# Last stage: a bank of its own for one sum, and another order of ScalarE's and VectorE's steps

## The chip, the cores and the metric

One Trainium2 chip; the kernel runs on one core. The time is the device time of the whole program in microseconds (us), the median of three runs. TensorE (PE) multiplies matrices into PSUM, eight banks of 128 x 512 fp32; VectorE (DVE) and ScalarE (ACT) read and empty them; GpSimd (POOL) and SyncE (SP) mostly issue transfers. Each engine runs its own list of instructions in order, and they wait for each other with semaphores.

## What is computed

The reference is two graph layers and two mixtures of experts over 10,000 rows of 512 features. The last stage is the second mixture, eight experts with 32 hidden units each, of which the two best count for a row:

```python
def _L1_ffn_ref(x, router_w, w1, b1, w2, b2, gamma, beta):
    logits = xf @ router_w
    gate_vals, idx = jax.lax.top_k(logits, K)        # K = 2
    gates = jax.nn.softmax(gate_vals, axis=-1)
    out = jnp.zeros_like(xf)
    for e in range(E):                               # E = 8
        h = jax.nn.relu(xf @ w1[e] + b1[e]) @ w2[e] + b2[e]
        y = _layernorm(xf + h, gamma[e], beta[e])
        w = jnp.sum(jnp.where(idx == e, gates, 0.0), axis=-1)
        out = out + w[:, None] * y
    return out.reshape(B, S, D)
...
    x = x + _L1_gnn_ref(_layernorm(x), ...)
    x = x + _L1_ffn_ref(_layernorm(x)[None], ...)[0]
    return x
```

## The kernel before

The last stage is `dense1_phase`. The rows are cut into 20 chunks `g` of 512 rows, each of four tiles `t` of 128 rows; the last chunk has three tiles. A fully unrolled loop of 21 rounds (`bodies`, `body(0, c_)`) runs on every engine, with the order of the steps written out by hand for each. In round `g` four chunks are in work: `front` is chunk g+2, whose rows are made ready (`scale_y`, `sum_`, `square`, variance); `mid` is chunk g+1, which is normalised (`norm`), turned by TensorE (`turn`), and split into a high and a low half (`high` on ScalarE, `low` on VectorE); `main` is the inner chunk g, with the hidden units (`up`, `hidden`, `hidden_high`, `hidden_low`), the variances of the experts (`cross`, `gram`, `quadratic`, `turn_squares`, `sum_squares`) and the routing; `behind` is chunk g-1, whose coefficients are made, turned and spread (`turn_coef`, `spread`, `scale`, `weighted_high`, `weighted_low`) and whose result is made (`product` on TensorE, `finish` on VectorE: a multiplication with `pox[t]` and an addition of `po1[t]`). `in_range` switches the four parts off at the ends. Every wide matmul is done in three (`split3`, lines 67 to 69), with high and low halves.

A product of 512 floats by 128 partitions fills a PSUM bank, and all eight are taken: `pu0`, `pu1`, `pq0`, `pq1`, `ptr`, `psm`, `pb`, `px`. From chunk 1 on all four turns of a chunk's rows use the one bank `ptr` (`turn_bank`): the turn of tile t+1 waits until tile t's low half is made (`xl_made`). The fourth tile's product uses the same two banks as the second's, `pb` and `px`, and waits for the second tile's `finish` (line 3424). The lists of `body` that matter: ScalarE's, from line 3003, and VectorE's, from line 3246.

The router's logits of the next chunk come out of `logits` (8 matmuls into `psm`), which waits for all four low halves. ScalarE's `small_copy` empties that bank, `turn_small` turns it, and `logits_of` reads it on VectorE. The variance of chunk g+2 (`variance_of`, line 3122) waits for all four of ScalarE's `square`; GpSimd's `power` follows it, and VectorE's `shifts` that. In the round, VectorE does `sum_squares`, `shifts`, `finish` 0, `variance`, `logits_of` and `finish` 1 to 3 after `variance_of`, in this order, and then `coefficients` and `routing` of the next round; ScalarE starts each round's work with `softmax_exp` (line 3001), which waits for the second step of `routing`.

Of the kernel before, what the change touches and what calls it, by code (L numbers as in the profile page):

```python
# [71 lines left out]
def tiles(g):  # L72

    return LAST if g == NG - 1 else T
# [2700 lines left out]
def dense1_phase(nc, a, k, ex, out):  # L2775
# [5 lines left out]
    with ExitStack() as stack:  # L2781
# [27 lines left out]
        coef_t = c.sb("coef_t", [P, GR], F32R)  # L2809
        pu, pq = ([c.ps(f"{n}{i}") for i in range(2)] for n in ("pu", "pq"))  # L2810
        ptr, psm, pb, px = (c.ps(n) for n in ("ptr", "psm", "pb", "px"))
        pox, po1 = [pu[0], pb, pq[0], pb], [pu[1], px, pq[1], px]

        NSHIFT, NCOEF, NVAR, NROUTE, EXP_STEP = 5, 8, 4, 10, 2
        consts, first_means = c.sem("consts"), c.sem("first_means")
# [27 lines left out]
        def in_range(i, c_, ahead):  # L2843

            return not isinstance(i, int) or 0 <= c_ + ahead < NG
# [82 lines left out]
        def _(act_):  # L2928
# [14 lines left out]
            def scale_y(i, c_, t):  # L2943

                g, u = i * XS + c_, c_ % XS
                act_.wait_ge(y_in[u][t], i * 16 + 16 * (c_ // XS + 1))
                if t == 0:
                    act_.wait_ge(gains, g + 1)
                act_.activation(x3[u][:, t, :], x3[u][:, t, :], ACT.Copy, scale=gain[:, t:t + 1]).then_inc(affine, 1)
# [25 lines left out]
            def high(g, n, t):  # L2975
                act_.wait_ge(turned, 4 * g + t + 1)
                act_.activation(xh[n][:, :, t * P:t * P + P], turn_bank(g, t)[:].rearrange("p (c n) -> p c n", n=P), ACT.Copy)\
                    .then_inc(xh_made, 1)
# [5 lines left out]
            def hidden_high(g, n, fc):  # L2984
                act_.wait_ge(hid_made, FC1 * g + fc + 1)
                act_.activation(hh[:, fc, cols(g)], hid[n][:, fc, cols(g)], ACT.Copy).then_inc(hh_made, 1)
# [5 lines left out]
            def small_copy(g):  # L2992
                act_.wait_ge(small_done, g + 1)
                for b, rows in enumerate((slice(0, HALF_P), slice(HALF_P, P))):
                    act_.activation(small_t[rows].rearrange("p (a n) -> p a n", a=2),
                                    psm[rows].rearrange("p (a b n) -> p a b n", a=2, b=2)[:, :, b, :], ACT.Copy)\
                        .then_inc(small_out, 1)
# [5 lines left out]
            def body(i, c_):  # L3003
                g, n, n1 = i * XS + c_, c_ % 2, (c_ + 1) % 2
                front, mid, main, behind = (in_range(i, c_, ahead) for ahead in (2, 1, 0, -1))
                if mid:
                    norm(i, c_ + 1, 0)
                    norm(i, c_ + 1, 1)
                if c_ == 0:
                    for t in range(T):  # L3010
                        half(i, 2, t)
                if main:
                    softmax_exp(g)
                    hidden(g, n, 0)
                if mid:
                    high(g + 1, n1, 0)
                if main:
                    hidden_high(g, n, 0)
                if mid:
                    norm(i, c_ + 1, 2)  # L3020
                    if tiles(g + 1) == T:
                        norm(i, c_ + 1, 3)
                if front:
                    scale_y(i, c_ + 2, 0)
                if main:
                    hidden(g, n, 1)
                    hidden_high(g, n, 1)
                if behind:
                    act_.wait_ge(coef_turned, g)
                    act_.activation(coef_t[:], px[:], ACT.Copy).then_inc(coef_out, 1)  # L3030
                if mid:
                    high(g + 1, n1, 1)
                if front:
                    scale_y(i, c_ + 2, 1)
                    scale_y(i, c_ + 2, 2)
                if mid:
                    high(g + 1, n1, 2)
                if behind:
                    weighted_high(g - 1, 0)
                if front:  # L3040
                    if tiles(g + 2) == T:
                        scale_y(i, c_ + 2, 3)
                    square(i, c_ + 2, 0)
                    square(i, c_ + 2, 1)
                if mid and tiles(g + 1) == T:
                    high(g + 1, n1, 3)
                if behind:
                    weighted_high(g - 1, 1)
                if front:
                    square(i, c_ + 2, 2)  # L3050
                    if tiles(g + 2) == T:
                        square(i, c_ + 2, 3)
                if mid:
                    small_copy(g + 1)
                if in_range(i, c_, 3):
                    for t in range(tiles(g + 3)):
                        half(i, c_ + 3, t)
# [25 lines left out]
        def _(v):  # L3083
# [162 lines left out]
            def body(i, c_):  # L3246
                g, n, n1 = i * XS + c_, c_ % 2, (c_ + 1) % 2
                front, mid, main, behind = (in_range(i, c_, ahead) for ahead in (2, 1, 0, -1))
                if behind:
                    coefficients(g - 1, n1, (c_ - 1) % XS)  # L3250
                if front:
                    mean_of(i, c_ + 2)
                if main:
                    routing(g, n)
                if mid:
                    low(g + 1, n1, 0)
                if main:
                    hidden_low(g, n, 0)
                if front:
                    sum_(i, c_ + 2, 0)  # L3260
                if main:
                    hidden_low(g, n, 1)
                if mid:
                    low(g + 1, n1, 1)
                if front:
                    sum_(i, c_ + 2, 1)
                if behind:
                    scale(g - 1, n1, 0)
                if mid:
                    low(g + 1, n1, 2)  # L3270
                if main:
                    quadratic(g, n, 0)
                if behind:
                    weighted_low(g - 1, 0)
                if front:
                    sum_(i, c_ + 2, 2)
                    if tiles(g + 2) == T:
                        sum_(i, c_ + 2, 3)
                if mid and tiles(g + 1) == T:
                    low(g + 1, n1, 3)  # L3280
                if behind:
                    scale(g - 1, n1, 1)
                if main:
                    quadratic(g, n, 1)
                if behind:
                    weighted_low(g - 1, 1)
                if front:
                    variance_of(i, c_ + 2)
                    if in_range(i, c_, 3):
                        gains_of(i, c_ + 3)  # L3290
                if main:
                    sum_squares(g, 0)
                    sum_squares(g, 1)
                if front:
                    shifts(i, c_ + 2)
                if behind:
                    finish(i, c_ - 1, 0)
                if main:
                    variance(g, n)
                if mid:  # L3300
                    logits_of(g + 1, n1)
                if behind:
                    for t in range(1, tiles(g - 1)):
                        finish(i, c_ - 1, t)
# [37 lines left out]
        def _(pe):  # L3342
            pe.wait_ge(consts, 6)

            def turn(g, t):
                pe.wait_ge(normed, 4 * g + t + 1)
                if g:
                    pe.wait_ge(xl_made, 4 * g + t)
                for kc in range(KC):
                    last = pe.transpose(turn_bank(g, t)[:, kc * P:kc * P + P], xf[:, t, kc * P:kc * P + P], k.ident[:])  # L3350
                last.then_inc(turned, 1)
# [63 lines left out]
            def product(g, t, main):  # L3415
                sl = slice(t * P, t * P + P)
                if t == 0:
                    pe.wait_ge(cl_made, FC1 * g + FC1)
                    if main:
                        pe.wait_ge(hid_made, FC1 * g + 2 * FC1)  # L3420
                if t == 2 and main:
                    pe.wait_ge(quad_summed, FC1 * g + 2 * FC1)
                if t == 3:
                    pe.wait_ge(mul_done, 8 * g + 4 + 16)
                pe.matmul(pox[t][:], coef_t[:, sl], ex.rows_x[:], start=True, stop=True).then_inc(x_done, 1)
                pe.matmul(po1[t][:], coef_t[:, sl], ex.rows_1[:], start=True, stop=False, skip_group_check=True)
                for fc in range(FC1):
                    last = split3(pe, po1[t][:], (ch[:, fc, sl], cl[:, fc, sl]),
                                  (ex.w2g[0][:, fc, :], ex.w2g[1][:, fc, :]), False, fc == FC1 - 1)
                last.then_inc(one_done, 1)  # L3430
# [157 lines left out]
```

## Time and profile before

| | us |
|---|---|
| median of 3 runs (lowest, highest) | 2427.51 (2425.49, 2428.58) |
| the profiled execution: its time | 2430.37 |
| the profiled execution: span from first to last instruction | 2428.6 |
| PE busy | 2278.6 (94%) |
| PE weight loads busy | 1824.9 (75%) |
| DVE busy | 1795.1 (74%) |
| ACT busy | 1152.4 (47%) |
| POOL busy | 676.4 (28%) |

The last stage takes from about 1881 to the end, some 547 us. Busy shares say how much of the span an engine executes something; matmuls overlap, so TensorE's share is not a share of its peak. In the timelines the number behind the start is the length of an operation as the profiler shows it; the next operation of the same engine may start before it has ended. The bracket at a row's end tells how long the engine was idle before and what ended that.

### The profile page before, as it was taken

How to read it: one execution, taken by the hardware profiler on the slowest of the kernel's cores; microseconds unless marked ns; L12 is line 12 of the kernel's file. 1: busy time of each engine (PE TensorE's matmuls, PEld its weight loads, DVE VectorE, ACT ScalarE, POOL GpSimd, SP SyncE). 2: the span in 40 equal slices, each digit the busy share in tenths (PEclk: the TensorE clock that was granted, in tenths of full speed). 3: DMA queues.
4: the chain of work that ended last, by engine and by line, in shares of the span. 5: the costliest groups of instructions: out<-in, count | busy, mean ns of one | idle time of the engine just before them, and what ended most of it. 6: DMA issues, size and time to landing. Idle time of an engine off the chain costs nothing. (4 is left out here: it accounts for less than half of the span.)

```text
span 2428.6 us, 33166 instructions
## 1 busy us (share of the span) xinstructions
PE 2278.6 (94%) x10610; PEld 1824.9 (75%) x10610; DVE 1795.1 (74%) x4258; ACT 1152.4 (47%) x2136; POOL 676.4 (28%) x624
## 2 busy tenths in 40 slices
PE   6799986899999999999789999999997899999998
PEld 4577664688888888888668788888876677777776
DVE  8588796888888888887556755555566688888886
ACT  7565422445455454554442222222235767667652
POOL 6455022222122221210232222122133434333310
PEclk9899987999999999999899999999999899999999
DMA  5221133132231322311453343433446566666631
GB/s 168 57 54 53 19 126 104 57 100 83 75 104 53 105 70 87 102 51 52 135 173 126 125 145 127 134 129 128 135 157 195 123 174 160 148 169 166 152 106 51
DMA packets 155873, 271.89 MB, mean 112 GB/s; under 512 B 35538, under 2 KB 36178, under 8 KB 155478
## 3 DMA queue, kind: packets, MB, share of 16 engines
q1 hardware_dynamic: 123014, 203.00, 25.1%
q0 software_dynamic: 32720, 67.19, 12.9%
q8 instruction: 68, 1.11, 0.2%
q14 instruction: 71, 0.58, 0.1%
HBM read 185.82 MB, written 100.41 MB: 118 GB/s over the span
## 5 line engine op out<-in xcount | busy, mean ns | idle before, releaser
L2417 ACT ACTIVATE conv_h<-conv_h 128x512 f32<-128x512 f32 x79 | 50.0, 632 | 305.9 <-DVE conv_h L2346 288.8
L2894 POOL DMA_INDIRECT next_own<-message,net_slot_d x75 | 123.7, 1650 | 155.4 <-DMA next_own<-own 138.1
L2315 DVE TENSOR_TENSOR conv_yl<-conv_pty,conv_yh 128x512 fp32r<-128x512 f32 x79 | 54.6, 692 | 150.2 <-ACT conv_yh L2407 140.9
L67 PE MATMUL conv_p<-conv_w_hi,conv_yh 128*128 128x512 f32 x316 | 132.2, 418 | 1.2 <-DVE conv_yl L2315 1.2
L1372 POOL TENSOR_TENSOR d_rs<-d_ve,net_half_neg 128x4 f32<-128x4 f32 x37 | 37.3, 1008 | 340.8 <-DVE d_ve L1430 283.4
L67 PE MATMUL d_po<-shared_wq_hi,d_hh 128*128 128x512 f32 x316 | 129.4, 409 | 0.0
L67 PE MATMUL d_pc<-d_xh,shared_wv_hi 128*128 128x512 f32 (+1 forms) x320 | 128.4, 401 | 0.0
L67 PE MATMUL d_pa<-d_xh,xp_w_hi 128*128 128x512 f32 (+1 forms) x320 | 127.6, 399 | 0.0
L69 PE MATMUL conv_p<-conv_w_hi,conv_yl 128*128 128x512 f32 x316 | 126.2, 399 | 0.0
L68 PE MATMUL conv_p<-conv_w_lo,conv_yh 128*128 128x512 f32 x316 | 126.0, 399 | 0.0
L69 PE MATMUL conv_p<-conv_w_hi,conv_hl 128*128 128x512 f32 x316 | 125.5, 397 | 0.0
L68 PE MATMUL conv_p<-conv_w_lo,conv_hh 128*128 128x512 f32 x316 | 124.5, 394 | 0.0
L67 PE MATMUL conv_p<-conv_w_hi,conv_hh 128*128 128x512 f32 x316 | 124.2, 393 | 0.2 <-DVE conv_hl L2315 0.2
L69 PE MATMUL d_pa<-d_xh,xp_w_lo 128*128 128x512 f32 (+1 forms) x320 | 124.3, 388 | 0.0
L69 PE MATMUL d_pc<-d_xh,shared_wv_lo 128*128 128x512 f32 (+1 forms) x320 | 124.1, 388 | 0.0
L68 PE MATMUL d_pa<-d_xl,xp_w_hi 128*128 128x512 f32 (+1 forms) x320 | 123.6, 386 | 0.0
L68 PE MATMUL d_pc<-d_xl,shared_wv_hi 128*128 128x512 f32 (+1 forms) x320 | 123.4, 386 | 0.0
L69 PE MATMUL d_po<-shared_wq_hi,d_hl 128*128 128x512 f32 x316 | 123.4, 390 | 0.0
L68 PE MATMUL d_po<-shared_wq_lo,d_hh 128*128 128x512 f32 x316 | 123.3, 390 | 0.0
L1023 POOL DMA_INDIRECT early_val<-values,net_slot_s x79 | 80.8, 1022 | 122.4 <-DVE d_x L1508 56.6
L2343 DVE SCALAR_TENSOR_TENSOR conv_h<-conv_p,conv_dg,conv_msg 128x512 f32<-128x512 f32 x79 | 59.3, 751 | 70.9 <-PE conv_p L69 47.6
L2286 POOL COPY conv_at<-net_slot_d 128x4 int32 (+1 forms) x20 | 4.7, 237 | 367.8 <-DVE conv_h L2346 346.7
(621 smaller groups left out, 7209.5 us busy)
## 6 DMA issues: line engine op xcount, KB each, us to landing
conv_yin<-y SPq DMA_DIRECT2D x79, 256.0 KB, 2.8
h<-conv_h SPq DMA_DIRECT2D x79, 256.0 KB, 2.0
own<-xp_own_buf SPq DMA_DIRECT2D x79, 256.0 KB, 2.0
next_own<-own SPq DMA_DIRECT2D x79, 256.0 KB, 4.3
next_x<-y SPq DMA_DIRECT2D x79, 256.0 KB, 3.8
out<-d_res SPq DMA_DIRECT2D x79, 256.0 KB, 2.7
y<-d_y SPq DMA_DIRECT2D x78, 256.0 KB
d_x<-in_x SPq DMA_DIRECT2D x10, 1024.0 KB, 7.3
```

What stands on the lines that cost most here:

```text
L67: te.matmul(out, lhs[0], rhs[0], start=first, stop=False, skip_group_check=True)
L68: te.matmul(out, lhs[0], rhs[1], start=False, stop=False, skip_group_check=True)
L69: return te.matmul(out, lhs[1], rhs[0], start=False, stop=last, skip_group_check=True)
L1023: pool.indirect_dma_start(early.val[:, t, :], None, k.values[:, :], bass.IndirectOffsetOnAxis(ap=k.slot["s"][:, T * g + t:T * g + t + 1], ...
L1372: pool.tensor_tensor(rs[n][:], ve[n][:], k.half_neg[:, 0:T], ALU.pow).then_inc(pow_done[n], 1)
L2286: pool.tensor_copy(at[:], k.slot["d"][:, ds(T * g, T)]).then_inc(at_made, 1)
L2315: v.tensor_tensor(lo[:, t % 2, :], bank[t % 2][:], hi[:, t % 2, :].bitcast(F32), ALU.subtract)\
L2343: v.scalar_tensor_tensor(h[:, t, :], p1[t % 2][:], dg[:, t:t + 1], msg[:, t, :], ALU.mult, ALU.add)\
L2417: act_.activation(h[:, t, :], h[:, t, :], ACT.Relu).then_inc(h_made, 1)
L2894: pool.indirect_dma_start(own[n][:, t, :], None, k.message2[:, :], bass.IndirectOffsetOnAxis(ap=k.slot["d"][:, T * g + t:T * g + t + 1], a ...
```

## The change

The fourth tile's second sum, `po1[3]`, goes into the bank `ptr` instead of `px`. The fourth tile's `product` waits for one step of `finish` less (only `pb` must be free), and the first turn of a chunk, from chunk 3 on, waits for the last `finish` of the chunk three before it. On ScalarE the second tile's high half comes ahead of the coefficients' copy and of the inner chunk's second `hidden_high`; the fourth tile's comes ahead of squares 0 and 1; `small_copy` comes ahead of square 3. On VectorE the second tile's low half and `sum_` 1 come ahead of the inner chunk's second `hidden_low`, and `sum_` 3 goes from before the fourth low half to just before the variance. No operation is added or taken away.

```diff
--- before.py
+++ after.py
@@ -2809,7 +2809,7 @@
         coef_t = c.sb("coef_t", [P, GR], F32R)
         pu, pq = ([c.ps(f"{n}{i}") for i in range(2)] for n in ("pu", "pq"))
         ptr, psm, pb, px = (c.ps(n) for n in ("ptr", "psm", "pb", "px"))
-        pox, po1 = [pu[0], pb, pq[0], pb], [pu[1], px, pq[1], px]
+        pox, po1 = [pu[0], pb, pq[0], pb], [pu[1], px, pq[1], ptr]
 
         NSHIFT, NCOEF, NVAR, NROUTE, EXP_STEP = 5, 8, 4, 10, 2
         consts, first_means = c.sem("consts"), c.sem("first_means")
@@ -3024,12 +3024,13 @@
                     scale_y(i, c_ + 2, 0)
                 if main:
                     hidden(g, n, 1)
-                    hidden_high(g, n, 1)
+                if mid:
+                    high(g + 1, n1, 1)
                 if behind:
                     act_.wait_ge(coef_turned, g)
                     act_.activation(coef_t[:], px[:], ACT.Copy).then_inc(coef_out, 1)
-                if mid:
-                    high(g + 1, n1, 1)
+                if main:
+                    hidden_high(g, n, 1)
                 if front:
                     scale_y(i, c_ + 2, 1)
                     scale_y(i, c_ + 2, 2)
@@ -3040,18 +3041,19 @@
                 if front:
                     if tiles(g + 2) == T:
                         scale_y(i, c_ + 2, 3)
+                if mid and tiles(g + 1) == T:
+                    high(g + 1, n1, 3)
+                if front:
                     square(i, c_ + 2, 0)
                     square(i, c_ + 2, 1)
-                if mid and tiles(g + 1) == T:
-                    high(g + 1, n1, 3)
                 if behind:
                     weighted_high(g - 1, 1)
                 if front:
                     square(i, c_ + 2, 2)
-                    if tiles(g + 2) == T:
-                        square(i, c_ + 2, 3)
                 if mid:
                     small_copy(g + 1)
+                if front and tiles(g + 2) == T:
+                    square(i, c_ + 2, 3)
                 if in_range(i, c_, 3):
                     for t in range(tiles(g + 3)):
                         half(i, c_ + 3, t)
@@ -3258,12 +3260,12 @@
                     hidden_low(g, n, 0)
                 if front:
                     sum_(i, c_ + 2, 0)
-                if main:
-                    hidden_low(g, n, 1)
                 if mid:
                     low(g + 1, n1, 1)
                 if front:
                     sum_(i, c_ + 2, 1)
+                if main:
+                    hidden_low(g, n, 1)
                 if behind:
                     scale(g - 1, n1, 0)
                 if mid:
@@ -3274,8 +3276,6 @@
                     weighted_low(g - 1, 0)
                 if front:
                     sum_(i, c_ + 2, 2)
-                    if tiles(g + 2) == T:
-                        sum_(i, c_ + 2, 3)
                 if mid and tiles(g + 1) == T:
                     low(g + 1, n1, 3)
                 if behind:
@@ -3285,6 +3285,8 @@
                 if behind:
                     weighted_low(g - 1, 1)
                 if front:
+                    if tiles(g + 2) == T:
+                        sum_(i, c_ + 2, 3)
                     variance_of(i, c_ + 2)
                     if in_range(i, c_, 3):
                         gains_of(i, c_ + 3)
@@ -3346,6 +3348,8 @@
                 pe.wait_ge(normed, 4 * g + t + 1)
                 if g:
                     pe.wait_ge(xl_made, 4 * g + t)
+                if g > 2 and t == 0:
+                    pe.wait_ge(mul_done, 8 * (g - 3) + 8 + 16)
                 for kc in range(KC):
                     last = pe.transpose(turn_bank(g, t)[:, kc * P:kc * P + P], xf[:, t, kc * P:kc * P + P], k.ident[:])
                 last.then_inc(turned, 1)
@@ -3421,7 +3425,7 @@
                 if t == 2 and main:
                     pe.wait_ge(quad_summed, FC1 * g + 2 * FC1)
                 if t == 3:
-                    pe.wait_ge(mul_done, 8 * g + 4 + 16)
+                    pe.wait_ge(mul_done, 8 * g + 3 + 16)
                 pe.matmul(pox[t][:], coef_t[:, sl], ex.rows_x[:], start=True, stop=True).then_inc(x_done, 1)
                 pe.matmul(po1[t][:], coef_t[:, sl], ex.rows_1[:], start=True, stop=False, skip_group_check=True)
                 for fc in range(FC1):
```

## Rows read from the trace of the kernel before

**Rows 1.** Windows between exponentials: length, ScalarE's exponential (count), granted clock, DMA share, GB/s
```profile
2027.83:2054.02 26.19, 0.23 (x2) 1.00 0.67 159
...
2080.26:2106.78 26.52, 0.23 (x1) 1.00 0.66 159
...
2159.26:2185.50 26.24, 0.23 (x1) 1.00 0.67 158
...
2342.83:2368.80 25.97, 0.23 (x2) 1.00 0.11 44
```

**Rows 2.** Waits of TensorE's weight loads, window 1945 to 2345: total, times, longest
```profile
PEld d_pb L3425 <- DVE d_res L3244: 8.5, 15, 0.9
PEld d_ptr L3350 <- issue: 6.5, 15, 0.4
```

**Rows 3.** Timeline of TensorE in one round: start, length, line, operation, tiles
```profile
2153.80 0.40 PE L69 MATMUL d_pq<-ex_w2g_hi,d_cl 128*128 128x512 f32 x1
...
2154.30 0.50 PE L3425 MATMUL d_pb<-ex_rows_x,d_coef_t 128*128 128x512 f32 x1
...
2162.67 0.60 PE L3350 MATMUL d_ptr<-net_ident,d_xf 128*128 128x128 f32 x4
...
2165.87 0.40 PE L3412 MATMUL d_pb<-d_coef_t,ex_spread 128*128 128x512 f32 x1
...
2166.31 0.63 PE L3350 MATMUL d_ptr<-net_ident,d_xf 128*128 128x128 f32 x4
...
2169.55 0.60 PE L3350 MATMUL d_ptr<-net_ident,d_xf 128*128 128x128 f32 x4
...
2171.65 0.47 PE L3357 MATMUL d_psm<-d_xh,ex_route 128*128 128x512 f32 x1
...
2173.34 0.39 PE L3359 MATMUL d_psm<-d_xl,ex_route 128*128 128x512 f32 x1
```

**Rows 4.** Timeline of ScalarE in the same round
```profile
2163.13 0.68 ACT L2982 ACTIVATE d_hid<-d_pu,ex_b 128x512 f32<-128x512 f32 x1
...
2164.85 0.59 ACT L2977 ACTIVATE d_xh<-d_ptr 128x512 fp32r<-128x512 f32 x1
...
2165.32 1.33 ACT L2949 ACTIVATE next_x<-next_x,d_gain 128x512 f32<-128x512 f32 x2
...
2173.38 0.71 ACT L2961 ACTIVATE d_squared<-next_x,d_less_mean 128x512 bf16<-128x512 f32 x1
...
2174.08 0.76 ACT L2995 ACTIVATE d_small_t<-d_psm 64x256 f32<-64x256 f32 x2
...
2174.87 0.63 ACT L2940 ACTIVATE next_own<-next_own 128x512 f32<-128x512 f32 x1
```

**Rows 5.** Timeline of VectorE from the same round
```profile
2156.47 0.69 DVE L3244 TENSOR_TENSOR d_res<-d_res,d_px 128x512 f32<-128x512 f32 x1 [0.23 <-PE d_px L69]
...
2161.53 0.69 DVE L3140 TENSOR_TENSOR d_xl<-d_ptr,d_xh 128x512 fp32r<-128x512 f32 x1
...
2166.08 0.69 DVE L3115 TENSOR_TENSOR next_x<-next_x,next_own 128x512 f32<-128x512 f32 x1
...
2170.81 0.69 DVE L3140 TENSOR_TENSOR d_xl<-d_ptr,d_xh 128x512 fp32r<-128x512 f32 x1
...
2174.21 0.17 DVE L3122 TENSOR_SCALAR d_ve<-d_square_sum 128x4 f32<-128x4 f32 x1 [0.72 <-ACT d_squared L2961]
...
2179.01 0.68 DVE L3241 TENSOR_TENSOR d_res<-next_x,d_pb 128x512 f32<-128x512 f32 x1
```

**Rows 6.** Timeline of VectorE in rounds 0 and 1
```profile
1911.88 0.69 DVE L3140 TENSOR_TENSOR d_xl<-d_ptr,d_xh 128x512 fp32r<-128x512 f32 x1 [0.66 <-ACT d_xh L2977]
...
1915.26 1.29 DVE L3158 TENSOR_REDUCE d_square_parts<-d_pq 128x16 f32<-128x512 f32 x2 [1.38 <-PE d_pq L3367]
...
1934.51 0.69 DVE L3140 TENSOR_TENSOR d_xl<-d_ptr,d_xh 128x512 fp32r<-128x512 f32 x1
...
1937.91 0.17 DVE L3122 TENSOR_SCALAR d_ve<-d_square_sum 128x4 f32<-128x4 f32 x1 [0.72 <-ACT d_squared L2961]
```

## Prediction

> **What bounds the kernel now.** Only the last stage is touched, so the first view is its table by chunk: stretches cut where ScalarE starts the exponential of a chunk, which happens once in each round of the loop [rows 1]. Fifteen rounds, from the round of chunk 2 to that of chunk 16, take 26.19 to 26.52 us, nearly all 26.2; the later ones, with no chunk left to load, take 25.97 and less. TensorE's granted clock is 1.00 in all of these stretches, its full 2.4 GHz. The second view is who waits for whom [rows 2]: TensorE's weight loads wait 15 times, 8.5 us in total, for the second sum of the second tile (`res + po1[1]`), and 15 times for the third row turn. These are the waits that the change goes for. The third view is the order of time in one round, TensorE [rows 3], ScalarE [rows 4] and VectorE [rows 5]. It shows that the two waits are not the bound but the place where a longer loop closes. I write E for the start of the exponential (2159.26) and count from it.
>
> The loop now: VectorE makes the first tile's low half at E+2.27; the turns follow at 2162.67, 2166.31 and 2169.55; the fourth tile's high half and then its low half at 2170.81 (E+11.55); then VectorE's weighting, ScalarE's high half of it, squares 2 and 3, and VectorE's variance at 2174.21 (E+14.95). From there VectorE is never idle until it starts the second tile's product at 2179.01 (4.80 later), and the rest of the four tiles, the coefficients and the head of routing bring the next exponential at 2185.50 (6.49 later). 14.95 + 4.80 + 6.49 = 26.24, the round of [rows 1]. So what the change is worth is what it does to these three legs.
>
> **Part 1, the bank.** The fourth tile's second product goes to `ptr`, and its wait asks for one VectorE step less: the product of the second tile, not the sum after it. On TensorE the two matmuls around this wait start 0.50 us apart (2153.80, 2154.30) against 0.23 to 0.24 without a wait (seven steps from the first route matmul, 2171.65, to the last, 2173.34), and the one after a wait is followed some 0.1 us late, so the stall costs 0.37 us of TensorE's time. If TensorE comes out of it earlier, VectorE's last sum loses its wait, shown as 0.23 [rows 5]; about 0.10 of it is the usual gap behind its own first operation, so I count 0.13. The third leg becomes 6.36. The new wait on the first turn asks for the fourth tile's sum. It is queued behind twelve matmuls of `up` and eight of the product; the sum ends 4.4 us after VectorE began the second tile's product (2156.47 + 0.69, less 2179.01 - 26.24), while TensorE restarts at about 0.74 and has twenty matmuls of 0.23 ahead of the turn, 5.4. That wait costs nothing; if its cover of 1.0 us were gone, TensorE would stand for what is missing.
>
> **Part 2, the second tile's halves.** ScalarE makes the second high half at 2164.85, 1.72 us after it started `hidden` (2163.13). Ahead of the coefficient copy and `hidden_high` it comes one operation, about 0.6 us, after it, so 1.1 us sooner, and its low half follows as much sooner. The third turn now waits: 2165.87 to 2166.31 is 0.44 against 0.23, 0.21 lost and 0.03 behind it. This stall goes. The coefficient copy comes 0.17 us sooner. `hidden_low` for the inner chunk goes behind `sum_` 1, which waits for `scale_y` 1 (2165.32, two in 1.33, so 0.71 long; perhaps 0.1 sooner then). So VectorE is held until about E+6.70 (now 2166.08, E+6.82), and everything that it did during that wait now stands behind it. From there to the fourth low half it has seven operations on 128x512: six at 0.61 apart and the quadratic at 0.66. Full-width operations in a row start 0.60 apart (two in 1.29 us, [rows 6]; each is 0.69 long). That makes E+11.0.
>
> **Where TensorE is by then.** The turn of the second tile needs the first low half: E+2.27 + 0.69 + 0.15 = E+3.11, with the 0.15 taken from the fourth low half's end (2171.50) and the first route matmul (2171.65). It stands at 2162.67 = E+3.41 now, and would be ready at about E+2.75, so this becomes a new stall. From this turn to the third: 3.64 now, less 0.21, plus 0.03 for the restart, 3.46, so E+6.57. To the fourth: 3.24, E+9.81. From it to the fourth low half as now, 2169.55 to 2170.81, 1.26: E+11.07. VectorE's own E+11.0 and TensorE's E+11.07 agree, so both ends of this bound lie close: the low half comes 0.5 us sooner than now.
>
> **Part 3, squares, the small copy and the fourth tile.** The high half moves ahead of squares 0 and 1; it must wait for its turn (E+10.44), and ScalarE idles for it. The squares fit behind it and end before the second weighting (E+11.07 + 0.61 + 0.69 = E+12.37). What matters is the swap of the last two: `small_copy` now stands ahead of square 3. It reads the logits, so it can't start before the route matmuls are done. From the fourth low half: 0.84 us to the first of them, 2.08 until the last (2173.34, 0.39 long) has ended, and 0.04 more; then the copy holds ScalarE for 0.79 (2174.08 to the next start, 2174.87), and from square 3's start to the variance on VectorE is 0.83 (2173.38 to 2174.21). Together 4.58 us. Now the way is through the weighting and squares 2 and 3, 2170.81 to 2174.21, 3.40 us. So the variance comes at E+11.07+4.58 = E+15.65 instead of E+14.95. `sum_` 3 is off this way: it is due about E+13.6, a microsecond before square 3 starts. Waiting behind square 3 on ScalarE are four halves and two norms, under 0.8 us each (2174.87 to 2179.7 now) and not needed before 2185.50, and behind the variance on VectorE all of the rest: GpSimd's power, the shifts, the sums of the tiles. No DMA is issued in this stretch by the moved steps; the loads of `own` wait for sums of the round before.
>
> **The sum.** A full round: 15.65 + 4.80 + 6.36 = 26.81, against 26.24, so +0.57. Fifteen such rounds: +8.5. In round 1 the turns come late for a reason that the change leaves alone (the second one behind the first low half), so I leave its fourth low half at 1934.51 [rows 6]: 1934.51 + 4.58 = 1939.09 against 1937.91, less 0.13: +1.05. Round 0: 1911.88, sooner by 0.34 of turn stall, plus 4.58 gives the variance at 1916.12 and the sums of squares at 1916.28 where they now start at 1915.26: +1.0. Round 17 [rows 1] has no fourth square or scaling, and there the halves and the bank gain their 0.5 to 0.7 us. Sum +8.5 + 1.05 + 1.0 - 0.6 = +9.9. Added to the profiled execution's 2430.4 that is 2440.3; it stands 2.9 above the median of the runs, 2427.5, so 2437.4 there. I say 2437.
>
> **Bounds.** The per-round term carries nearly all. If the 0.15 and 0.04 of signalling are smaller in the new order and the restart costs nothing, the round is +0.35, sum +6.6. If VectorE loses another gap and the power's turn on GpSimd adds one, +0.75, sum +12.6. The first two rounds may add or save 1 us. Most of this is 2432 to 2440.
>
> **Rivals.** (A) Faster: square 3 isn't held by the copy, because the logits come much sooner than I reckon. Then the variance stays 3.40 behind the low half: 11.07 + 3.40 + 4.80 + 6.36 = 25.63, -0.61 for 16 rounds and a little at the end, about 2417. TensorE's own work allows it: 26.24 less the stalls 0.37 and 0.24 is 25.63 too. It decides at a low half 1.18 us sooner than now, since the new way is 4.58 and the old 3.40; both engines' sums give only 0.5. The Trainium skill ("Perfetto Trace Analysis", Optimization Strategy) reads the same gap repeating on the engine that should be saturated as a possible lack of PSUM space. By that rule the extra bank is the cure and this rival's time is the result; the rows say the gap is set by VectorE's start at 2179.01, which the bank doesn't move. Chance 8%. (B) No change: parts 1 and 2 gain what part 3 loses, 0.5 against 0.7, if VectorE's leg from the variance has slack that I don't see, such as a power that is waited for. Within 0.2%, about 2428. Chance 12%. (C) The forecast, 80%; the lower end of it, +4 to +5 us, counts as no change.
>
> A difference below about 0.2% (4.9 us) can't be told from none here. Slower by more 0.77, within 0.15, faster 0.08. Case A alone lies far off the range and B a little, so the range stays with the forecast and part of B: 2430 to 2441.
>
> **What would show it.** In the changed profile: rounds of about 26.8 between exponentials; ScalarE idle before `small_copy` (some 0.4 us, ended by TensorE's route matmuls), then the copy, then square 3, then the variance at E+15.6; the fourth low half at E+11.05; TensorE waiting about 0.35 us before the second turn for the first low half and about 0.65 before the fourth product, now for the second tile's product; no wait before the third turn. I am wrong if the fourth low half comes before E+10.4, if the copy starts before E+13.5, or if the variance is seen at or before E+15.

## The result

The changed kernel takes 2440.24 us, median of 5 runs (2437.39 to 2442.70), against 2427.51 for the kernel before, median of 5 as well (2425.49 to 2428.58). The ratio is 1.005, 95% interval 1.0038 to 1.0061: slower by half a per cent. The forecast was 2437, with a range of 2430 to 2441. The profiled execution spans 2438.5 us, 9.9 more than the 2428.6 of before.

The busy times on the page of the changed kernel are almost those of before; nothing on it but the span tells of a change:

```profile
span 2438.5 us, 33166 instructions
...
PE 2278.6 (93%) x10610; PEld 1825.7 (75%) x10610; DVE 1792.3 (74%) x4258; ACT 1152.1 (47%) x2136; POOL 672.8 (28%) x624
```

The rounds, cut at the exponentials as in [rows 1] (window, length, ScalarE's exponential and its count, granted clock, DMA share, GB/s):

```profile
1921.74:1950.13 28.39, 0.23 (x1) 0.94 0.47 94
1950.13:1976.93 26.80, 0.23 (x1) 1.00 0.65 163
...
2164.97:2191.76 26.79, 0.23 (x2) 1.00 0.66 156
...
2352.48:2377.83 25.35, 0.23 (x1) 1.00 0.12 46
```

The full rounds take 26.8 us, where they took 26.2 in [rows 1]. Fifteen of them, 1950.13 to 2352.48, are 402.35 us. The last row, round 17, is shorter than its 25.97 of before.

The waits in those fifteen rounds, for all engines (total us, times, longest):

```profile
DVE d_ve L3124 <- ACT d_squared L2961: 20.1, 15, 1.4
...
PEld d_pb L3429 <- DVE d_res L3243: 14.8, 15, 1.3
...
ACT d_small_t L2995 <- PE d_psm L3363: 4.6, 15, 0.3
...
PE d_ptr L3354 <- DVE d_xl L3142: 2.5, 14, 0.4
```

The line numbers are those of the changed kernel. The fourth product (L3429) still waits in every round, longer than in [rows 2] (14.8 us for 8.5), now for the product of the second tile (L3243) where it was the sum (L3244). The variance (`d_ve`) waits 1.34 us each time for a square, against 0.72 in [rows 5]. ScalarE waits for the route matmuls before it can copy the logits, and TensorE has a new wait for the first low half. One round, which starts at E = 2164.97, in order of time:

```profile
2168.08 0.63 PE L3354 MATMUL d_ptr<-net_ident,d_xf 128*128 128x128 f32 x4 [0.17 <-DVE d_xl L3142]
...
2171.54 0.60 PE L3354 MATMUL d_ptr<-net_ident,d_xf 128*128 128x128 f32 x4
...
2171.64 0.69 DVE L3117 TENSOR_TENSOR next_x<-next_x,next_own 128x512 f32<-128x512 f32 x1 [0.93 <-ACT next_x L2949]
...
2175.38 0.60 ACT L2977 ACTIVATE d_xh<-d_ptr 128x512 fp32r<-128x512 f32 x1 [0.56 <-PE d_ptr L3354]
...
2176.01 0.69 DVE L3142 TENSOR_TENSOR d_xl<-d_ptr,d_xh 128x512 fp32r<-128x512 f32 x1
...
2176.84 0.47 PE L3361 MATMUL d_psm<-d_xh,ex_route 128*128 128x512 f32 x1
...
2178.60 0.69 DVE L3117 TENSOR_TENSOR next_x<-next_x,next_own 128x512 f32<-128x512 f32 x1
...
2178.97 0.78 ACT L2995 ACTIVATE d_small_t<-d_psm 64x256 f32<-64x256 f32 x2 [0.30 <-PE d_psm L3363]
...
2179.77 0.72 ACT L2961 ACTIVATE d_squared<-next_x,d_less_mean 128x512 bf16<-128x512 f32 x1
...
2180.62 0.17 DVE L3124 TENSOR_SCALAR d_ve<-d_square_sum 128x4 f32<-128x4 f32 x1 [1.34 <-ACT d_squared L2961]
...
2185.41 0.68 DVE L3243 TENSOR_TENSOR d_res<-next_x,d_pb 128x512 f32<-128x512 f32 x1
```

Read from the top: the second turn at E+3.11, held by the first low half; the third turn at E+6.57; `sum_` 1 at E+6.67, behind VectorE's wait of 0.93 for `scale_y` 1; the fourth low half at E+11.04; then the chain that is new. The first route matmul comes at +0.83, the copy when they are done, square 3 behind the copy, the variance at E+15.65. Next to it stands `sum_` 3 at 2178.60, which becomes important in the first experiment.

### The profile page after: what moved, and what is told of

Same layout as the page of the kernel before. It is cut to its first block and busy times, and to the rows that moved or that the text cites. A ratio compares the mean times of both kernels' runs of the same rounds, so it can differ in the third digit from the quotient of the medians.

```text
span 2438.5 us, 33166 instructions
## 1 busy us (share of the span) xinstructions
PE 2278.6 (93%) x10610; PEld 1825.7 (75%) x10610; DVE 1792.3 (74%) x4258; ACT 1152.1 (47%) x2136; POOL 672.8 (28%) x624
```

## The experiments

Each run stands against its own runs of the kernel before on the same chip, since that kernel itself had medians between 2427.5 and 2437.9 us from one chip to another. The length of a full round is the sharper measure, though each kernel has a profile of one execution only. Within a kernel it repeats to 0.07 us, but for one or two rounds that are 0.2 to 0.3 longer in every one of them; it is given without those. No kernel leaves out any part of the computation; only orders, waits and one bank differ.

**Copy back.** One edit of the changed kernel undone.

```diff
                     square(i, c_ + 2, 2)
-                if mid:
-                    small_copy(g + 1)
                 if front and tiles(g + 2) == T:
                     square(i, c_ + 2, 3)
+                if mid:
+                    small_copy(g + 1)
```

> The changed kernel with one edit undone: small_copy stands behind square 3 again. Theory (the copy holds square 3 back, and with it the variance): the fourth low half stays at E+11.05, the variance comes 3.40 behind it at E+14.45, the full rounds shorten from 26.8 to 25.6 us, and the kernel takes about 2417 us, some 10 less than before the change. Rival (the loss comes from VectorE's new order around hidden_low or from the bank's new wait): rounds stay at 26.7 to 26.8, about 2439 us.

Measured: 2439.62 against 2437.94, ratio 1.0008 (0.9999 to 1.0017); rounds of 26.34. Neither theory has that. The waits of this kernel, total, times and longest:

```profile
ACT d_squared L2961 <- DVE next_x L3117: 9.8, 15, 0.7
```

and the place in its timeline, in a round that starts at 2193.66:

```profile
2207.29 0.68 DVE L3117 TENSOR_TENSOR next_x<-next_x,next_own 128x512 f32<-128x512 f32 x1
...
2208.01 0.72 ACT L2961 ACTIVATE d_squared<-next_x,d_less_mean 128x512 bf16<-128x512 f32 x1 [0.66 <-DVE next_x L3117]
...
2208.85 0.17 DVE L3124 TENSOR_SCALAR d_ve<-d_square_sum 128x4 f32<-128x4 f32 x1 [0.88 <-ACT d_squared L2961]
```

Square 3 waits for its own sum now. `sum_` 3 starts at E+13.63, as in the changed kernel, and there the copy had covered it. So the change holds square 3 twice, and the copy is only the later of the two: undoing it gives back 0.45 of the 1.2 us. I had reckoned with one.

**The copy alone**, in the kernel before (the same two steps swapped the other way).

> The kernel before with one edit alone: small_copy ahead of square 3. Theory: the fourth low half stays at E+11.55, the variance moves to 4.58 behind it, E+16.13, rounds of 27.4 us instead of 26.24, the whole about 2448 us (15 rounds of +1.17, +2.9 in rounds 0 and 1). Rival (the copy is harmless): 26.24, 2427 us.

Measured: 2457.91 against 2437.94, ratio 1.0091 (1.0076 to 1.0107), 20 us more; rounds of 27.45, with the fourth low half at E+11.55 and the variance at E+16.16. It is the costliest edit: alone it takes 1.2 us a round, since there nothing brings the low half sooner.

**The bank alone**, in the kernel before:

```diff
-        pox, po1 = [pu[0], pb, pq[0], pb], [pu[1], px, pq[1], px]
+        pox, po1 = [pu[0], pb, pq[0], pb], [pu[1], px, pq[1], ptr]
...
+                if g > 2 and t == 0:
+                    pe.wait_ge(mul_done, 8 * (g - 3) + 8 + 16)
...
-                    pe.wait_ge(mul_done, 8 * g + 4 + 16)
+                    pe.wait_ge(mul_done, 8 * g + 3 + 16)
```

> The kernel before with the bank alone: po1[3] in ptr, both waits as in the change, both orders as before. Theory: TensorE's stall of 0.37 us goes, but only the 0.13 of VectorE's last sum shortens the round, to 26.1 us; about 2425 us. Rival (TensorE's stall was the bound): rounds of 25.87 us, about 2421.5 us.

Measured: 2433.45 against 2437.94, ratio 0.9985 (0.9976 to 0.9994); rounds of 26.09 (26.06 to 26.10, one of 26.41). The length of the round decides for the theory, 26.11 by the prediction's sum against 25.87; the time, 4.5 us less with an interval from 1.5 to 5.8, holds the theory's 2.5 and has the rival's 6 just outside. TensorE's stall of 0.37 us was mostly slack.

**No bank** in the changed kernel, the three edits above undone.

> The changed kernel with the bank undone (po1[3] in px, waits as before), both new orders kept. Theory: the fourth product starts 0.8 us later after VectorE's start of the second tile, so the second turn comes at E+3.41 instead of 3.11, the fourth low half at E+11.31 and the variance at E+15.89; with the 0.13 back in VectorE's last sum, rounds of 27.2 us, about 2443 to 2446 us. Rival (the bank doesn't matter here, or its new wait costs): 26.8 us or less.

Measured: 2453.76 against 2437.94, ratio 1.0065 (1.0050 to 1.0081); rounds of 27.22. With both new orders the bank is worth 0.42 us a round, three times what it is worth alone. There the second turn follows the fourth product (E+3.44 without the bank, E+3.11 with it), and the third turn follows the second at 3.42 to 3.46 in both.

**Copy and sum back.** In the changed kernel `small_copy` goes behind square 3, and:

```diff
                     sum_(i, c_ + 2, 2)
+                    if tiles(g + 2) == T:
+                        sum_(i, c_ + 2, 3)
                 if mid and tiles(g + 1) == T:
                     low(g + 1, n1, 3)
...
                 if front:
-                    if tiles(g + 2) == T:
-                        sum_(i, c_ + 2, 3)
                     variance_of(i, c_ + 2)
```

> The changed kernel with two edits undone: small_copy behind square 3, and sum_ 3 right behind sum_ 2, ahead of the fourth low half. Theory after the first study (square 3 was held twice, by the copy and by its own sum): nothing holds square 3, but sum_ 3 pushes the fourth low half on VectorE from E+11.04 to E+11.56; the variance comes 3.40 behind it, E+14.96, and rounds are 26.1 us, the whole 3 us less than the kernel before. Rival (something else holds the round at 26.3): no shorter than 26.3 us.

Measured: 2426.12 against 2428.78, ratio 0.9986 (0.9977 to 0.9996), 2.7 us less; rounds of 26.07.

**The sum between.** `small_copy` behind square 3, and `sum_` 3 between the second weighting and the second quadratic:

```diff
                 if behind:
                     scale(g - 1, n1, 1)
+                if front and tiles(g + 2) == T:
+                    sum_(i, c_ + 2, 3)
                 if main:
                     quadratic(g, n, 1)
```

> The changed kernel with small_copy behind square 3 and sum_ 3 on VectorE between the second weighting and the second quadratic. Theory: the fourth low half stays at E+11.04, sum_ 3 is done at about E+12.9, before square 3 could start (E+13.6), the variance comes at E+14.44, and rounds are 25.6 us; TensorE's own 25.5 to 25.6 is then the bound. About 10 us less than the kernel before. Rival: 26.1 to 26.3 us, 2 us less at most.

Measured: 2418.15 against 2428.78, ratio 0.9951 (0.9937 to 0.9965), 10.6 us less; rounds of 25.6.

**Low half first.** As with copy and sum back, and on VectorE besides:

```diff
                     low(g + 1, n1, 1)
+                if main:
+                    hidden_low(g, n, 1)
                 if front:
                     sum_(i, c_ + 2, 1)
-                if main:
-                    hidden_low(g, n, 1)
```

> The changed kernel with small_copy behind square 3, sum_ 3 right behind sum_ 2, and hidden_low 1 ahead of sum_ 1, in VectorE's wait for scale_y 1. Theory: VectorE is 0.6 us sooner from sum_ 1 on, so that sum_ 3 fits ahead of the fourth low half, which TensorE's turn holds at E+11.04; variance at E+14.44, rounds of 25.6 us, as far below the kernel before as the one with sum_ 3 between, 10 us. Rival (VectorE's order of hidden_low is of no account): 26.1 us, as with two edits undone.

Measured: 2415.81 against 2428.78, ratio 0.9939 (0.9926 to 0.9953), 13 us less; rounds of 25.6. The last two agree in the rounds and can't be told apart in time. The wait for `scale_y` 1 now has `hidden_low` in it, and the sum that had to go behind the fourth low half fits ahead of it. The timeline of a round that starts at 2178.00:

```profile
2188.45 0.60 ACT L2977 ACTIVATE d_xh<-d_ptr 128x512 fp32r<-128x512 f32 x1 [1.20 <-PE d_ptr L3354]
...
2189.08 0.69 DVE L3142 TENSOR_TENSOR d_xl<-d_ptr,d_xh 128x512 fp32r<-128x512 f32 x1
...
2191.64 0.71 ACT L2961 ACTIVATE d_squared<-next_x,d_less_mean 128x512 bf16<-128x512 f32 x1
...
2192.35 0.77 ACT L2995 ACTIVATE d_small_t<-d_psm 64x256 f32<-64x256 f32 x2
...
2192.47 0.17 DVE L3124 TENSOR_SCALAR d_ve<-d_square_sum 128x4 f32<-128x4 f32 x1 [0.72 <-ACT d_squared L2961]
```

and all waits of its TensorE loads over some twelve rounds:

```profile
PEld d_psm L3361 <- issue: 3.7, 13, 0.3
PEld d_ptr L3354 <- issue: 0.5, 2, 0.3
```

The fourth low half is at E+11.08, as in the changed kernel, and the variance 3.39 behind it, at E+14.47. The fourth product waits no more; what is left is a short wait before the route matmuls.

**The second tile's halves alone**, in the kernel before (ScalarE's and VectorE's moves around the second tile; bank, fourth tile and copy as they were).

> The kernel before with the second tile's halves alone: high 1 ahead of the coefficient copy and hidden_high 1, low 1 and sum_ 1 ahead of hidden_low 1; bank and all the rest as before. Theory: TensorE's stall of 0.24 us at the third turn goes, but ScalarE's first weighted half comes 0.4 us later behind VectorE's later scale, and squares 0 and 1, still ahead of the fourth high half, push that to about E+11.2 and the fourth low half to E+11.8; rounds of 26.5 us, 3 to 4 us more than before. Rival (the stall was the bound): 26.0 us, 3.5 us less.

Measured: 2432.07 against 2428.78, ratio 1.0009 (0.9999 to 1.0018); rounds of 26.44. The fourth high half stands at 2196.92 in a round that starts at 2185.75, E+11.17, behind two squares:

```profile
2195.50 0.71 ACT L2961 ACTIVATE d_squared<-next_x,d_less_mean 128x512 bf16<-128x512 f32 x1
...
2196.21 0.71 ACT L2961 ACTIVATE d_squared<-next_x,d_less_mean 128x512 bf16<-128x512 f32 x1
...
2196.92 0.57 ACT L2977 ACTIVATE d_xh<-d_ptr 128x512 fp32r<-128x512 f32 x1
```

A move that ends a wait of TensorE lengthens the round by 0.2 us. The time can't be told from that of before; the rounds can. With the fourth tile's high half moved as well and the bank given, it is 26.07 (copy and sum back); no run separates those two.

**The fastest without the bank.** The version with the low half first, and the bank undone.

> The fastest version so far (small_copy behind square 3, sum_ 3 behind sum_ 2, hidden_low 1 ahead of sum_ 1) with the bank undone: po1[3] in px, waits as before. Theory: the fourth product starts 0.8 us behind the point where the bank allows it, the second turn comes at E+3.41, the fourth low half at E+11.31, the variance at E+14.71, and with 0.13 back in VectorE's last sum rounds are 26.0 us; about 4 us less than the kernel before. So the bank is worth 0.38 us a round here, against 0.13 to 0.15 alone. Rival (the bank is worth the same everywhere): 25.75 us.

Measured: 2424.44 against 2430.02, ratio 0.9976 (0.9967 to 0.9985), 5.6 us less; rounds of 25.99 (25.96 to 26.02). The bank is worth 0.38 us a round here.

**Squares turned first.** The version with the low half first, and on TensorE:

```diff
                     gram(g, 1)
+                    turn_squares(g, 0)
                     if mid:
                         pe.wait_ge(logit_made, 2 * g + 2)
                         logits(g + 1, n1)
-                    for fc in range(FC1):
-                        turn_squares(g, fc)
+                    turn_squares(g, 1)
```

> The same fastest version, with the bank, and on TensorE the turning of the first half of the squares moved ahead of the route matmuls. Theory (TensorE is the bound now, and its last wait, for the fourth low half before the route matmuls, costs 0.12 us): rounds of 25.49 us instead of 25.61, no wait before the route matmuls; 1.8 us less in all, too little to tell in the time. Rival (VectorE or ScalarE still set the round): 25.6 us, or more because small_copy comes later.

Measured: 2419.42 against 2430.02, ratio 0.9949 (0.9935 to 0.9963); rounds of 25.57. All waits of TensorE's loads over twelve rounds:

```profile
PEld d_ptr L3354 <- ACT d_xf L2972: 0.4, 1, 0.4
PEld d_ptr L3354 <- issue: 0.3, 1, 0.3
PEld d_pb L3429 <- DVE d_res L3243: 0.2, 1, 0.2
```

The wait before the route matmuls is gone, and TensorE has gained by it what the theory says: from the start of the last matmul of `gram` to that of the first product of the rows it takes 2.87 us, against 3.00 with the low half first, and the first turn starts at E-0.57 for E-0.47. Yet the round is shorter by 0.04 and not by 0.12, because the second turn now stands behind the first low half in every round:

```profile
2206.40 0.69 DVE L3142 TENSOR_TENSOR d_xl<-d_ptr,d_xh 128x512 fp32r<-128x512 f32 x1
...
2206.77 0.60 PE L3408 MATMUL d_px<-net_ident,d_parts 128*128 128x128 f32 x4
2207.24 0.63 PE L3354 MATMUL d_ptr<-net_ident,d_xf 128*128 128x128 f32 x4
```

It starts 0.15 us after the low half has ended (0.22 with the low half first), which is the signalling time of the prediction, and so small a wait that the view of waits lists it for TensorE's matmuls once. From there the loop runs through the three engines: the second turn at E+3.11, the third at 6.57, the fourth low half at 11.04, the variance at 14.44, the second tile's product at 19.23, the next exponential at 25.58. So with the low half first TensorE's own work was the longer by 0.04 us (25.62), and here that loop is the bound. The rival, that VectorE or ScalarE set the round at 25.6, describes this kernel; the theory described the one before it.

All rounds together; "halves" is the second tile's, "low" is `hidden_low` 1 ahead of `sum_` 1:

| kernel | bank | halves | fourth high half first | copy | `sum_` 3 | round, forecast | round, measured |
|---|---|---|---|---|---|---|---|
| before | no | no | no | last | early | | 26.2 |
| bank alone | yes | no | no | last | early | 26.1 | 26.1 |
| second halves alone | no | yes | no | last | early | 26.5 | 26.4 |
| copy alone | no | no | no | ahead | early | 27.4 | 27.45 |
| changed | yes | yes | yes | ahead | last | 26.8 | 26.8 |
| no bank | no | yes | yes | ahead | last | 27.2 | 27.2 |
| copy back | yes | yes | yes | last | last | 25.6 | 26.3 |
| copy and sum back | yes | yes | yes | last | early | 26.1 | 26.1 |
| sum between | yes | yes | yes | last | middle | 25.6 | 25.6 |
| low first | yes | yes | yes, low | last | early | 25.6 | 25.6 |
| low first, no bank | no | yes | yes, low | last | early | 26.0 | 26.0 |

Squares turned first, which differs only on TensorE, is not in the table: 25.5 by the forecast, 25.6 measured. Of the ten forecasts of a round copy back missed by 0.7, and the others by less than 0.1.

## Why the prediction held, and where it did not

**The three legs.** The forecast for a full round was 15.65 + 4.80 + 6.36 = 26.81. In the round shown above it is 15.65 (2164.97 to 2180.62), 4.79 (to 2185.41) and 6.35 (to the next exponential, 2191.76): 26.79. The method, to follow one chain through three engines with the durations and gaps of the rows, was good to 0.02 us, because no step changed its length.

**Part 1.** The last sum's wait is gone and gave its 0.13. The bank alone shows it: 26.09 for 26.11. That the stall of 0.37 would not be saved was right. The new wait on the first turn showed nowhere: in the changed kernel the fourth tile's last sum ends at 2162.87 and that turn starts at 2164.12.

**Part 2.** The second turn waits for the first low half at E+3.11, as said, and the third turn comes at E+6.57, unhindered. `sum_` 1 at E+6.67 (6.70) and the fourth low half at E+11.04 (VectorE's 11.0, TensorE's 11.07). That the halves alone would be a loss stood in no part of the prediction; it was found in setting up that run.

**Part 3.** The 4.58 us from the fourth low half to the variance was 4.61 (2176.01 to 2180.62). The cause named there, that the copy waits for the route matmuls and square 3 for the copy, is confirmed by the copy alone, +1.22 a round for +1.18. The wait before the fourth product is there too: its first matmul starts 0.92 behind the one ahead of it (2158.43, 2159.35), 0.69 more than without a wait, for 0.65.

**The step that failed** is in the same part: "`sum_` 3 is off this way". It is off only as long as the copy hides it. I checked it against square 3's late start and did not go on to ask what comes last without the copy. The forecast for the changed kernel didn't need that answer. So rival A's 25.63 for a square not held by the copy was wrong: that kernel has 26.34. With both holds gone the rounds are 25.6, rival A's number, by a condition it didn't have.

**The other terms.** Fifteen rounds: 402.35 less 393.65 (1949.18 to 2342.83 in the trace of before) is +8.7, for 8.5. Round 1: 28.39 against 27.34, +1.05 as forecast. Round 17: -0.6 as forecast. Round 0: 22.54 against 21.14, +1.4 for 1.0. Its variance came at E+15.46 as forecast (E+15.42), but the sums of squares 0.51 behind it, where I had taken 0.16 from a full round. The end of the kernel, behind the last exponential, was 0.9 us longer, and the first exponential came 1.5 us sooner, 1.4 of it before the stage's first matmul, where no edit reaches. So the span's +9.9 equals my sum because errors of about 1.5 us cancel, which is luck. The medians lie 12.7 apart. The 2.8 us beyond the span's 9.9 lie with the kernel before: its profiled execution took 2430.37, 2.9 above its median, and that of the changed kernel took 2440.27, as its median. I had taken these 2.9 off the sum's 2440.3, and by them the forecast of 2437 fell 3.2 short. What put that one execution above its fellows is open; beside the experiments the same kernel had medians of 2428.78, 2430.02 and 2437.94.

**Round 1** came out for a wrong reason. I took its turns to be late because the second stands behind the first low half. But the second turn came at E+3.15 there, sooner than in a full round of the kernel before (E+3.43). It is the third that was late, at E+8.20, because TensorE ran at the lower clock between the two (last section). The clock fell in the same place in the changed kernel, and so its fourth low half stayed where I had left it (E+12.64 for E+12.67).

**The rule on repeating gaps.** The Trainium skill ("Perfetto Trace Analysis", Optimization Strategy) takes a gap that repeats on the engine that should be saturated as a possible lack of PSUM space. In the kernel before the bank gave 0.14 of a gap of 0.37, so there the rule pointed at a symptom. In the changed kernel the same bank gave 0.42, and with the low half first 0.38 (25.6 against 26.0). The condition is not a short loop, since the changed kernel's rounds are longer than those of before. It is what the third turn waits for. With the bank alone the second turn comes at E+3.16 instead of E+3.43, but the third stays at E+7.05: it is held by the second low half, which ends at E+6.90. Where the second tile's halves come first, that low half ends at E+5.75, and the 0.3 us that the bank gives the second turn pass on to the third turn and, where VectorE isn't later, to the fourth low half. The trace agrees with the rule only under that condition.

## What to carry to other kernels

A wait on the busiest engine shows where a loop closes and not which part of it is long. Follow one round from a fixed event back to itself through every engine, and give an edit the difference that it makes to that chain. A buffer is worth what is left of its gain at the next wait of the chain. When a held step is freed, ask at once what holds it next: here the same square was held by a copy and, hidden behind it, by its own sum. An engine's wait in the middle of its list is a place to put a step that is due later, as `hidden_low` into the wait for `scale_y`; the same step behind that wait cost the place of `sum_` 3.

## What the runs showed of the hardware

TensorE's granted clock in the first two rounds of the stage differs from one profiled execution to another. Each kernel has one, so what follows compares single executions. The rows are windows over round 1, as in [rows 1]. The kernel before:

```profile
1921.84:1949.18 27.34, 0.23 (x1) 0.94 0.49 104
```

Copy back:

```profile
1929.68:1956.06 26.38, 0.23 (x2) 1.00 0.53 108
```

The sum between, and the low half first:

```profile
1919.98:1947.16 27.18, 0.23 (x1) 0.94 0.50 106
```

```profile
1921.51:1947.10 25.59, 0.23 (x1) 1.00 0.53 110
```

A mean of 0.94 means that part of the round ran at 1.2 GHz and the rest at 2.4. The matmuls show which part; these are four of round 1 in the kernel before, 0.43 us apart in the first pair and 0.23 in the second:

```profile
1926.94 0.63 PE L67 MATMUL d_pq<-d_xh,ex_w2t_hi 128*128 128x512 f32 x1
1927.37 0.63 PE L68 MATMUL d_pq<-d_xl,ex_w2t_hi 128*128 128x512 f32 x1
...
1928.65 0.40 PE L68 MATMUL d_pq<-d_xl,ex_w2t_hi 128*128 128x512 f32 x1
1928.88 0.40 PE L69 MATMUL d_pq<-d_xh,ex_w2t_lo 128*128 128x512 f32 x1
```

The slow ones lie between the second and the third turn. In all seven kernels with 0.94 in round 1 the fourth low half came at E+12.64 to 12.67, whatever their order, and the round took 1.1 to 1.6 us more than a plain full round of the same kernel. In the five with 1.00 the low half came at E+11.06 to 11.77 and the round took at most 0.04 us more than a full one. The sum between and the low half first have the same full rounds, and their rounds 1 differ by 1.6 us.

In copy back, no bank, the fastest without the bank and squares turned first the clock was lower in round 0 (0.85 or 0.86 for 0.95 to 0.98), and round 0 took 23.4 to 25.3 us for 20.8 to 22.9. Their orders differ as well, so how much of this is the clock is not separated. No bank had both, 0.86 in round 0 and 0.94 in round 1. What decides where the clock is low was not tried.
